# A transformer layer on one core: tokens packed into seven sets behind the attention, first loads issued from two queues, products placed in the first waits

## The reference

```python
h = einsum('bnp,dp->bnd', patches(x), W) + b     # 16 images, 49 patches each of 768 numbers -> 256
h = concatenate([cls_tok, h], axis=1)            # 16 x 50 tokens of 256: 800 tokens
h = h + attention(layernorm(h))                  # 16 heads of 16; softmax over 50 keys; then Wo, bo
h = h + ffn(layernorm(h))
# ffn: relu(x @ w1.T + b1) -> fp8 (1024 wide) ; @ fp8(w2).T + b2, rounded to f16
```

## Time and profile before

| what | value |
|---|---|
| runs | 113.27, 112.28, 112.2 us; median 112.28 |
| profiled execution | 112.6 us, span of the instructions 110.8 us |
| busy | PE 102.9 (93%), DVE 67.2, POOL 52.1, ACT 48.4 us |
| chain that ended last | PE 86%, DMA 4%, DVE 2%, issue 2% |
| granted TensorE clock | 1.0 in the whole span |
| bytes moved | 12.59 MB; 363 to 401 GB/s from the third to the sixth fortieth of the span |

### The profile page before, as it was taken

How to read it: one execution, slowest core, us unless ns; L and a number is a source line. 1 busy time by engine, 2 the same in 40 slices (tenths; PEclk the granted TensorE clock), 3 DMA queues, 4 the chain that set the end, 5 groups by cost and what they waited for, 6 DMA issues and landing times.

```text
span 110.8 us, 3809 instructions
## 1 busy us (share of the span) xinstructions
PE 102.9 (93%) x1532; PEld 85.7 (77%) x1532; DVE 67.2 (61%) x128; ACT 48.4 (44%) x108; POOL 52.1 (47%) x94
## 2 busy tenths in 40 slices
PE   6997999999999979999899999999999999999940
PEld 6786766687767967798798998998897889799830
DVE  5001778595559779489989599688690644410140
ACT  0402110068906861568165347557549263446400
POOL 8791201649967506955938208208323344620040
PEclk9999999999999999999999999999999999999999
DMA  3899997588229415140331130240321002021012
GB/s 81 227 363 401 401 397 265 180 119 314 114 37 290 172 50 103 52 44 10 105 38 49 71 37 30 87 43 13 103 28 12 6 12 62 14 73 32 0 41 70
DMA packets 18785, 12.59 MB, mean 114 GB/s; under 512 B 13968, under 2 KB 15920, under 8 KB 18512
## 3 DMA queue, kind: packets, MB, share of 16 engines
q1 hardware_dynamic: 17868, 11.63, 36.2%
q10 hardware_dynamic: 900, 0.72, 2.2%
HBM read 9.07 MB, written 3.28 MB: 111 GB/s over the span
## 4 chain that ended last, share of the span: by engine, by line
PE 86%; DMA 4%; DVE 2%; issue 2%; SPq 2%; ACT 1%; ACTq 0%
PE psum L377 14%; PE psum L350 8%; PE psum L351 7%; PE psum L352 7%; PE psum L460 7%; PE psum L526 7%; PE psum L579 6%; PE psum L503 6%; PE psum L555 6%; PE psum L483 5%; PE psum L439 5%; DMA x_sb<-in_xt 4%; PE psum L442 3%; PE psum L538 2%; PE psum L406 2%
## 5 line engine op out<-in xcount | busy, mean ns | idle before, releaser
L377 PE MATMUL psum<-x_sb,w_sb 128*128 128x294 f32 (+1 forms) x72 | 18.8, 403 | 0.9 <-DVE qkv_sb L713 0.4
L947 ACT ACTIVATE hq<-psum,cols 128x300 fp8e4<-128x300 f32 (+1 forms) x24 | 11.6, 485 | 17.2 <-PE psum L555 9.1
L1071 POOL TENSOR_SCALAR var_eps<-mv 128x1 f32<-128x1 f32 x16 | 3.6, 225 | 28.4 <-DVE mv L775 16.5
L377 PEld LDWEIGHTS psum<-x_sb,w_sb 128*128 128x128 f32 x72 | 13.2, 201 | 3.9 <-DMA x_sb<-in_xt 1.3
L713 DVE SCALAR_TENSOR_TENSOR qkv_sb<-psum,rstd,bqkv_sb 128x768 f32<-128x768 f32 x8 | 8.1, 1018 | 5.1 <-PE psum L439 2.2
L913 ACT ACTIVATE probs<-shifted 128x400 f32<-128x400 f32 x16 | 7.8, 531 | 7.5 <-DVE shifted L749 7.5
L738 DVE TENSOR_REDUCE rmax<-psum 128x16 f32<-128x800 f32 x8 | 7.9, 982 | 4.7 <-PE psum L460 4.7
L789 DVE TENSOR_TENSOR x_sb<-psum,b_q 128x256 f16<-128x256 f32 x8 | 3.4, 423 | 11.9 <-PE psum L579 11.7
L350 PE MATMUL psum<-xn2T_hi,w_hi 128*128 128x300 f32 x32 | 10.5, 327 | 0.1
L1114 POOL TENSOR_TENSOR vals<-att,rsum 128x256 f32<-128x256 f32 x8 | 4.9, 618 | 10.2 <-DVE rsum L760 10.2
L351 PE MATMUL psum<-xn2T_lo,w_hi 128*128 128x300 f32 x32 | 9.6, 301 | 0.0
(11 more groups left out here) (81 smaller groups left out, 224.3 us busy)
## 6 DMA issues: line engine op xcount, KB each, us to landing
v_rows<-qkv_sb SPq DMA_DIRECT2D x32, 75.0 KB
x_sb<-in_xt SPq DMA_DIRECT2D x6, 294.0 KB, 8.3
w_sb<-in_w1t SPq DMA_DIRECT2D x1, 1024.0 KB, 6.1
w_sb<-in_w2t SPq DMA_DIRECT2D x1, 1024.0 KB, 5.6
v_sb<-v_rows SPq DMA_DIRECT2D x16, 50.0 KB
wqkv_sb<-in_wqkvt SPq DMA_DIRECT2D x2, 384.0 KB, 5.6
wqkv_r<-in_wqkv_rows SPq DMA_DIRECT2D x1, 768.0 KB, 7.4
out<-x_sb SPq DMA_DIRECT2D x26, 25.0 KB
```

The lines of the kernel that those rows point to most:

```text
L377: last = pe.matmul(dst, w_sb[:, k, m * P:(m + 1) * P], x_sb[b][:, k, :], start=(k == 0), stop=(k == KP - 1))
L947: act.activation(hq[:, m, a:b].rearrange("p t j n -> p (t j) n")[:, :, 0:QTOK], p_wide[:, ff1_bank[n], 0:(b - a) * TILE].rearrange("p (q n ...
```

## The change

Four edits come together.

1. **Seven sets.** Behind the attention the 800 tokens are cut into seven sets without gaps (`SETS`: 100, 100, 120, 120, 120, 120, 120). `valsT`, `xn2T` and `hq` are plain columns 0 to 799. `project`, `turn2`, `ff2`, and the VectorE, ScalarE and GpSimd work of the second layernorm and of the output are done once for a set, on `size(d)` partitions, in the stage after the tile in which the set ends (`ENDS` = tiles 0, 1, 3, 4, 5, 6, 7). FB is now sets 0-1, 2-3, 4-6: 200, 240 and 360 columns. The residual lies by quads and is needed by sets, so SP copies it from SBUF to SBUF: 4 transfers for each of tiles 0, 1, 2 and 7, 5 for tiles 3 to 6 (36 in all), of 5 to 25 rows. The zeroing of `valsT` and `hq` goes.
2. **Two queues at the start.** The four pieces of the first patches are all issued by ScalarE's queue, the four pieces of weights by SP's.
3. **Products in the first waits.** `patch(1, 0)` with k = 0 stands ahead of `mean_of_tokens`, and `turn_h0(1)` directly behind `turn_h0(0)`. Batch 2's second half is done in two parts, 196 columns in stage 2 and 98 in stage 3, where `turn_vals(2)` now stands behind `turn_probs(3)`.
4. **Moved work.** The table of pieces of `ff1`: six instead of eight in stages 4 to 6, four in stage 7 as before, fourteen behind instead of twelve. On VectorE `measure1` stands ahead of `maxima`, and `measure2` right behind `add_attention`. Stores: one for a set, the last set's in two halves of 64 and 56 rows on SP and ScalarE.

The diff, cut to what the prediction speaks of:

```diff
@@ -43,7 +43,11 @@
 PB = [(0, 2), (2, 5), (5, 8)]
-FB = [(0, 2), (2, 5), (5, 8)]
+FB = [(0, 2), (2, 4), (4, 7)]
+SETS = [(0, 100), (100, 200), (200, 320), (320, 440), (440, 560), (560, 680), (680, 800)]
+ENDS = [(b - 1) // TILE for a, b in SETS]
...
+def moves(t):
+    found = []
+    for j in range(QUADS):
+        first = t * TILE + j * QTOK
+        for d, (a, b) in enumerate(SETS):
+            z, e = max(a, first), min(b, first + QTOK)
+            if z < e:
+                found.append((32 * j + z - first, e - z, d, z - a))
+    return found
...
-        ff1_at = {4: [0], 5: [3], 6: [6], 7: [8, 9, 10, 11]}
-        ff1_mid = {4: [1, 2], 5: [4, 5], 6: [7]}
-        ff1_bank = [1, 0, 1, 1, 0, 1] + [(n + 1) % 2 for n in range(6, KF * len(FB))]
...
+        ff1_at = {4: [0], 5: [2], 6: [4], 7: [6, 7, 8, 9]}
+        ff1_mid = {4: [1], 5: [3], 6: [5]}
+        ff1_bank = [(n + 1) % 2 for n in range(KF * len(FB))]
...
-            load_w(0)
-            for c in range(1, len(CHUNKS[0])):
+            for c in range(len(CHUNKS[0])):
                 load_w(c)
-                load_x(0, c)
+            load_x(1, 0)
             for k in range(KD):
                 sp.dma_start(wqkv_sb[:, k, :], wqkvt[:, k, :]).then_inc(wqkv_in[k], 16)
-            load_x(1, 0)
...
@@ -334,15 +397,18 @@
                 elif t == 1:
                     sp.dma_start(w2_sb[:, :, :], w2t).then_inc(w2_in, 16)
-            for t in range(TILES):
-                if t < TILES - 1:
-                    sp.wait_ge(out_done, t + 1)
-                else:
-                    sp.wait_ge(last_done, 1)
-                for j in range(QUADS if t < TILES - 3 else QUADS // 2):
-                    store_out(sp, t, j)
-            for stored in out_stored:
-                sp.wait_ge(stored, 16 * QUADS * (TILES // 4))
+                sp.wait_ge(h0bo_done, t + 1)
+                for row, n, d, to in moves(t):
+                    sp.dma_start(h1[to:to + n, d], h0_bo[row:row + n, t]).then_inc(h0_in[d], 16)
+            last = len(SETS) - 1
+            for d in range(last):
+                sp.wait_ge(out_done, d + 1)
+                store_out(sp, d, 0, size(d))
+            sp.wait_ge(last_done, 1)
+            store_out(sp, last, 0, 64)
+            for q in range(4):
+                sp.wait_ge(out_stored[q], 16 * all_stored(q))
...
             def patch(b, m, ks):
-                n = cols_of(b)
-                dst = psum[:, patch_bank(b, m), 0:n]
+                part = slice(0, cols_of(b))
+                if b == 2 and m >= 1:
+                    part = slice(0, CUT) if m == 1 else slice(CUT, cols_of(b))
+                half = min(m, 1)
+                dst = psum[:, patch_bank(b, m), part]
...
-            def project(t):
-                if t == 0:
+            def project(d):
+                a, b = SETS[d]
+                if d == 0:
                     pe.wait_ge(wo_in, 16)
-                pe.wait_ge(valsT_done, t + 1)
+                pe.wait_ge(valsT_done, ENDS[d] + 1)
                 for k in range(KD):
-                    last = pe.matmul(p_proj, valsT[:, t % 2, k].rearrange("p j n -> p (j n)"), wo_sb[:, k, :],
+                    last = pe.matmul(psum[0:size(d), 7, 0:D], valsT[:, k, a:b], wo_sb[:, k, :],
                                      start=(k == 0), stop=(k == KD - 1))
                 last.then_inc(pe_proj, 1)
...
             for c, (a, z) in enumerate(CHUNKS[0]):
                 for m in range(KD):
                     patch(0, m, range(a, z))
+            patch(1, 0, range(0, 1))
             mean_of_tokens()
             turn_h0(0)
-            patch(1, 0, range(0, 2))
+            turn_h0(1)
+            patch(1, 0, range(1, 2))
             qkv(0, 0)
             qkv(0, 1)
-            turn_h0(1)
             patch(1, 0, range(2, KP))
             patch(1, 1, range(0, 1))
...
@@ -620,7 +693,7 @@
                     if 3 <= i <= 5:
                         turn_h0(i + 2)
                     qkv(i + 1, 0)
-                    if i >= 3:
+                    if i > 3:
                         turn_vals(i - 1)
...
@@ -631,33 +704,39 @@
                 turn_probs(i, 0)
                 turn_probs(i, 1)
                 if i == 2:
-                    patch(2, 1, range(0, KP // 2))
+                    patch(2, 1, range(0, 4))
+                if i <= 3:
                     turn_vals(i - 1)
-                    patch(2, 1, range(KP // 2, KP))
-                project(i - 1)
+                if i == 2:
+                    patch(2, 1, range(4, KP))
+                if i == 3:
+                    patch(2, 2, range(0, KP))
+                if set_ending(i - 1) is not None:
+                    project(set_ending(i - 1))
                 if i + 1 == TILES:
                     ff2(0, i)
                 attend(i)
                 for n in ff1_mid.get(i, []):
                     ff1(n, i + 1)
-                turn2(i - 2)
+                if set_ending(i - 2) is not None:
+                    turn2(set_ending(i - 2))
+            ff1(10, TILES)
+            ff1(11, TILES)
+            turn_vals(TILES - 1)
             ff1(12, TILES)
-            ff1(13, TILES)
-            turn_vals(TILES - 1)
+            project(6)
+            turn2(5)
+            for n in range(13, 16):
+                ff1(n, TILES)
             ff2(1, TILES)
-            turn2(TILES - 2)
-            project(TILES - 1)
-            for n in range(14, 16):
-                ff1(n, TILES)
+            turn2(6)
             ff2(2, TILES)
             ff2(3, TILES)
-            turn2(TILES - 1)
-            ff2(4, TILES)
             for n in range(16, 24):
                 ff1(n, TILES)
-            for t in range(5, TILES):
-                ff2(t, TILES)
+            for d in range(4, 7):
+                ff2(d, TILES)
...
                 if i >= 3:
                     turn_att(i - 1)
                     invert(i - 1)
+                if 4 <= i < TILES - 1:
+                    measure1(i + 1)
+                    gather1(i + 1)
                 maxima(i)
                 shift(i, 0)
                 shift(i, 1)
@@ -831,42 +916,44 @@
                     scale_qkv(3)
                     turn_att(1)
                     invert(1)
-                measure2(i - 2)
-                if i + 2 < TILES:
-                    measure1(i + 2)
-                gather2(i - 2)
-                if i + 2 < TILES:
-                    gather1(i + 2)
-                if i in (5, 6):
-                    low_turned2(i - 3)
+                    measure2(0)
+                    gather2(0)
+                if i == 6:
+                    low_turned2(2)
                 if 3 <= i < TILES - 1:
                     scale_qkv(i + 1)
                 if i + 1 < TILES:
                     turn_q(i + 1)
                     turn_k(i + 1)
-                add_attention(i - 1)
+                if i == 2:
+                    measure1(4)
+                    gather1(4)
+                if set_ending(i - 1) is not None:
+                    add_attention(set_ending(i - 1))
+                    measure2(set_ending(i - 1))
+                    gather2(set_ending(i - 1))
                 if i == 6:
...
-                    act.wait_ge(pool_init, 5)
-                act.activation(hq[:, m, a:b].rearrange("p t j n -> p (t j) n")[:, :, 0:QTOK],
-                               p_wide[:, ff1_bank[n], 0:(b - a) * TILE].rearrange("p (q n) -> p q n", n=QTOK), ACT.Relu, bias=b1_col[:, m:m + 1], saturate=False).then_inc(hq_done, 1)
-            act.dma_start(x_sb[0][:, piece(0, 0), :], xt[0][:, piece(0, 0), :]).then_inc(x_in[0][0], 16)
+                act.activation(hq[:, m, first:end], p_wide[:, ff1_bank[n], 0:end - first], ACT.Relu,
+                               bias=b1_col[:, m:m + 1], saturate=False).then_inc(hq_done, 1)
+            for c in range(len(CHUNKS[0])):
+                act.dma_start(x_sb[0][:, piece(0, c), :], xt[0][:, piece(0, c), :]).then_inc(x_in[0][c], 16)
             act.dma_start(cols[:, :], columns).then_inc(cols_in, 16)
             act.dma_start(ident, identity).then_inc(ident_in, 16)
...
-                if i == 2:
+                if i <= 3:
                     copy_vals(i - 1)
-                    embed(2, 1)
-                normalise2(i - 2)
+                    embed(2, i - 1)
+                d = set_ending(i - 2)
+                if d is not None:
+                    normalise2(d)
                 for n in ff1_mid.get(i, []):
                     relu(n)
-                high_turned2(i - 2)
+                if d is not None:
+                    high_turned2(d)
...
-            for n in range(12, 14):
+            relu(10)
+            normalise2(5)
+            relu(11)
+            copy_vals(TILES - 1)
+            relu(12)
+            high_turned2(5)
+            for n in range(13, 16):
                 relu(n)
-            normalise2(TILES - 2)
-            copy_vals(TILES - 1)
-            high_turned2(TILES - 2)
```

(36 more changed lines are left out.)

302 lines of the change are left out of this document (164 added, 138 removed).

## The result

| | before | changed kernel |
|---|---|---|
| median of 4 runs each | 112.36 us | 118.05 us |
| lowest, highest | 112.20, 113.27 | 117.00, 119.69 |
| ratio, 95% interval | | 1.0458 [1.0346, 1.057] |
| profiled execution, span | 112.6, 110.8 | 118.57, 116.8 |
| forecast | | 109.5 (108.5 to 112.0) |

The change makes the kernel slower by 4.6%, where the forecast was 2.5% faster.

The account below looks back on a forecast made before the run. TensorE's own steps and few waits were taken to bound the kernel. Work -1.83, start waits -1.18, stage 3 gap -0.47, new waits +1.0, end -0.3: -2.8 from 112.28 to 109.5; own range 108.5 to 110.6, 8 in 10 108.5 to 112.0.

Parts of the forecast that it names:

- SP's queue: 36 residual copies, 1.4 to 2.4 us of issue for a tile, ahead of the next values: 0, bound 2.
- Rival 1: SP's copies make `attend(1)` or `attend(3)` or both wait, together 1.4 to 2.5 us: 110.9 to 112.0; chance 0.12.
- The start: First patches come earlier and the idle time before the mean is filled: waits shrink by 1.18 us.
- First loads: Patches on ScalarE's queue beside SP's weights, third piece issued about 1 us earlier: gain 0.64, bounds 0 and 0.84.
- rival 4: Bytes limit the start: first pieces come no earlier, the two records filled in wait too; 110.7, chance 0.07.
- The wait for the mean: 0.64 us of TensorE idle before the mean is filled by two patch records at 0.268: -0.54.
- Removed work: TensorE: projection -0.88, `ff2` -0.88, `turn2` transposes -0.38, batch 2's narrow patches +0.31; together -1.83 us.
- Rivals 2 and 3: f32r with 240 columns costs the f32 price, about 125, chance 0.08; narrow `ff2` weights load slowly, 113.9, chance 0.05.
- rival 3: `ff2` weight loads slow at 100 or 120 columns, fast load needing 128 non-f32 weights: +4.4, 113.9; chance 0.05.
- The new waits: TensorE waits: `turn2(1)` +0.4, stage 4 +0.1, `project(6)` +0.25, `turn2(6)` +0.25; together +1.0 us.
- the end: Behind the last sum, SP and ScalarE issue one store each instead of two: -0.3 us.

Follow-up runs that it names:

- the first two experiments: Changed kernel with its 36 residual copies left out: 111.51 us; with them issued between the next tile's value stores and the wait for their landing: 111.74 us.
- the kernel with the old start: Changed kernel with the residual copies issued in the wait for the value stores' landing and the whole start as before: 110.87 us, ratio 0.9831.

## Why the prediction was wrong

**The step that failed: "SP's queue"**, put into the sum with 0 and bounded by 2. It was worth 6.3 to 6.5 us (the first two experiments). Three things were wrong in it.
- *The price.* I took 0.36 to 0.49 us for a copy from the rows of `v_rows`, as nearest in size and number. They go from SBUF to DRAM. A copy within SBUF costs 0.69, so five take 3.7, not 2.4. No row of before had that form; the bound above should have been far wider. The Trainium skill (DMA: Bandwidth & Descriptors, Anatomy of one DMA — SWDGE (gpsimd) path) says of a transfer issued by GpSimd that "the fixed cost is dominated by completion latency, not setup latency". These copies are issued by SP, and what they cost is their issue: 0.69 us of the queue each, while in the changed kernel's trace no engine waited for their landing.
- *The balance.* I set each tile's copies against that tile's slack once. A queue that is late by some amount in each round is later in each round. The right sum is the loop: 1.5 + 3 to 4 + 0.9 + 3.7 = 9.3 and more, against stages of 7.5 (58.97 - 51.48). With my own price it is 1.7 + 2.9 + 0.9 + 2.4 = 7.9 by tile 3, no shorter than a stage either: that would have been the warning.
- *What a wait brings behind it.* 2.86 us idle, and then about 7 us at the lower clock. No rival held that. It was not an additional cost, though: at `attend(7)` the late queue would have held TensorE anyway, and the executions took 117.00 us at a mean clock of 0.966 and 117.53 at 1.0.

Rival 1 ("SP's copies delay the values", 0.12) was the mechanism; its size, 110.9 to 112.0, came from the same price.

**The start** was the second step that failed. It was forecast with -1.18; instead the mean starts 1.17 later (11.59, 10.42), and at the first attend 0.88 of it is left against the kernel with the old start (30.01 to 29.13). "First loads" brought nothing, as rival 4 had it (third piece at 6.54 to 7.54, before 6.83 to 6.94). The DMA engines' share of 1.01 in 2 to 10 us speaks for its reason, bytes; no run tests that alone. "The wait for the mean" grew although two records filled it, since I had not followed `cols` on ScalarE's queue. The new start alone, queues and products together, cost 0.5%.

**What held.** Removed work and its steps. 28 records of wo's product at 0.22, 10 + 4 transposes at 0.105, 56 of `ff2` at 0.11, f32r at 0.11 for 240 and 0.165 for 360 columns, in the changed kernel's chain:

```profile
95.38 0.11 PE psum L416
...
96.06 0.88 PE psum L600 x4
96.93 0.21 PE psum L613 x2
...
100.84 1.75 PE psum L651 x16
...
102.76 0.17 PE psum L417
```

and the narrow patches and `ff2`'s weight loads, by shape (busy us, mean ns of one):

```profile
L446 PE MATMUL psum<-x_sb,w_sb 128*128 128x98 f32 x12 | 1.6, 279 | 0.1
...
L651 PEld LDWEIGHTS psum<-w_q,hq 128*120 128x120 fp8e4 x40 | 4.4, 133 | 0.2
```

The patches stood from 51.24 to 52.79, the last one's end included: (1.55 - 0.28) / 11 = 0.115 from start to start. Rivals 2 and 3 are thus refuted. By the Trainium skill's rule in rival 3 fast weight load is off for 100 or 120 columns. The trace agrees in direction: the loads got longer with fewer columns, 133 and 125 ns beside 98 with 128, though not twice as long, and not the 100 ns for 120 columns either. `ff2` steps at 1.75 / 16 = 0.109 as it did with 128 (0.110), so the longer loads were hidden.

**The new waits** were mis-sized by little; in the kernel with the old start `turn2(1)` waited 0.2 where I had 0.4, `turn2(6)` 0.2 where I had 0.25, and `scores(6)` 0.35, which I had not seen. With the failed terms left out (start -1.18, SP's queue 0) the sum was -1.6; the kernel with the old start measures -1.9 [-2.4, -1.4] (its ratio on 112.64). In its profiled execution the last product ends 1.2 earlier than before (105.33, 106.55), against the 1.3 of the terms, and 0.7 more is gained behind it, against 0.3 for "the end". (One slip in the prediction: 109.5 - 1.2 and + 1.0 are 108.3 and 110.5, not 108.5 and 110.6; nothing hangs on it.)
